# Seven-product columns widened from 512 to 680, over chains of two PSUM banks, in a quantised-weight FFN kernel

## What is computed

```python
lora_delta = lora_B @ lora_A * (LORA_ALPHA / LORA_RANK)
normalized = (weight + lora_delta).reshape(O, I // GROUP, GROUP) / scale
idx = jnp.searchsorted(thresholds, normalized, side='left')
w_eff = (cb[idx] * scale).reshape(O, I) + lora_delta
c = x @ w_eff.T                      # the conditioning product
result = jnp.einsum('bsd,od->bso', c, W_base) + b_base
ax, probs = einsum(c, A_w), softmax(einsum(c, router_w))
x = x + result + einsum(mixed(ax, probs, cores), B_w) * SCALING
```

## Time and profile before

| | |
|---|---|
| median of 3 runs | 2316.75 us (2315.3 to 2317.07) |
| the profiled execution's own time | 2317.91 us |
| its span, first to last instruction | 2316.1 us |
| mean granted clock of TensorE | 0.993 |
| PE busy, share of the span | 97% |
| DVE busy, share of the span | 85% |
| pairs 2 to 14 of stage 1, 13 pairs | 938.42 to 1213.16 us |

### The profile page before, as it was taken

How to read it: one execution, slowest core, us unless ns; L and a number is a source line. 1 busy time by engine, 2 the same in 40 slices (tenths; PEclk the granted TensorE clock), 3 DMA queues, 4 the chain that set the end, 5 groups by cost and what they waited for, 6 DMA issues and landing times.

```text
span 2316.1 us, 31908 instructions
## 1 busy us (share of the span) xinstructions
PE 2240.4 (97%) x11610; PEld 2022.0 (87%) x11610; DVE 1969.0 (85%) x2509; ACT 1496.5 (65%) x1962; POOL 1381.3 (60%) x894
## 2 busy tenths in 40 slices
PE   3889899999999999999999999999999999999999
PEld 2445479999999989899999989899999999999998
DVE  8999998889997977999997988999996766777776
ACT  7999978989886765666664865666663664122121
POOL 6888846669874534888775635887872132333231
PEclk9999999999999999999999999999999999999999
DMA  5787855444434434666664334666656666646554
GB/s 208 261 287 274 313 211 178 163 147 156 149 129 141 116 109 177 234 239 248 246 229 156 116 105 173 226 247 253 248 211 201 186 189 186 240 190 229 194 218 155
DMA packets 133234, 459.63 MB, mean 198 GB/s; under 512 B 14114, under 2 KB 66914, under 8 KB 96354
## 3 DMA queue, kind: packets, MB, share of 16 engines
q1 hardware_dynamic: 133076, 457.59, 56.7%
HBM read 306.41 MB, written 151.13 MB: 198 GB/s over the span
## 4 chain that ended last, share of the span: by engine, by line
PE 85%; DVE 9%; ACT 3%; DMA 1%; issue 1%; POOL 0%; DVEq 0%; SPq 0%; POOLq 0%; ACTq 0%
PE m L1239 6%; PE m L1238 6%; PE m L1240 6%; DVE acc L1713 6%; PE m L1190 5%; PE m L1192 5%; PE m L1191 5%; PE m L1296 4%; PE m L1298 4%; PE m L1297 4%; PE m L1346 4%; PE m L1348 4%; PE m L1347 4%; PE m L1131 4%; PE m L1307 3%; PE m L1306 3%
## 5 line engine op out<-in xcount | busy, mean ns | idle before, releaser
L1713 DVE SCALAR_TENSOR_TENSOR acc<-mk,dj,acc 128x1024 f32<-128x1024 uint8 x736 | 943.2, 1282 | 66.3 <-ACT mk L1461 47.9
L1461 ACT ACTIVATE mk<-wr,bj 128x1024 uint8<-128x1024 f32 x736 | 811.7, 1140 | 3.0 <-DVE acc L1713 2.1
L2034 POOL TENSOR_TENSOR pp<-pp,tm 128x1024 f32<-128x1024 f32 x184 | 454.0, 2468 | 22.3 <-POOL tm L2020 0.6
L2020 POOL TENSOR_SCALAR tm<-mp,dj 128x1024 f32<-128x1024 uint8 x192 | 226.0, 1178 | 211.0 <-ACT mp L1467 203.5
L1817 DVE TENSOR_TENSOR kl<-kw,kh 128x416 fp32r<-128x416 f32 (+3 forms) x310 | 237.6, 775 | 85.8 <-ACT kh L1496 84.7
L1496 ACT ACTIVATE kh<-kw 128x416 fp32r<-128x416 f32 (+3 forms) x310 | 169.1, 548 | 182.1 <-DMA kw<-in_wb 91.8
L1239 PE MATMUL m<-gl,xh 128*128 128x384 f32 (+2 forms) x800 | 280.9, 351 | 0.0
L1238 PE MATMUL m<-gh,xh 128*128 128x384 f32 (+2 forms) x800 | 280.6, 351 | 0.0
L1240 PE MATMUL m<-gh,xl 128*128 128x384 f32 (+2 forms) x800 | 279.8, 350 | 0.0
L1467 ACT ACTIVATE mp<-wr,bj 128x1024 uint8<-128x1024 f32 x224 | 255.1, 1139 | 0.0
L1773 DVE TENSOR_TENSOR part<-m,part 128x512 f32<-128x512 f32 (+4 forms) x362 | 217.6, 610 | 30.9 <-PE m L1240 16.6
(11 more groups left out here) (249 smaller groups left out, 5169.8 us busy)
## 6 DMA issues: line engine op xcount, KB each, us to landing
part<-part SPq DMA_DIRECT2D x191, 1036.0 KB, 4.8
rows<-in_wb SPq DMA_DIRECT2D x61, 1036.0 KB, 4.8
out<-part SPq DMA_DIRECT2D x31, 1024.0 KB, 4.8
kw<-in_ws SPq DMA_DIRECT2D x128, 208.0 KB, 2.7
xw<-in_x SPq DMA_DIRECT2D x96, 256.0 KB, 3.3
kw<-in_wb SPq DMA_DIRECT2D x92, 192.0 KB, 2.4
wr<-in_w SPq DMA_DIRECT2D x32, 512.0 KB, 5.9
dl<-delta SPq DMA_DIRECT2D x30, 512.0 KB, 5.3
```

Of the source, the lines that this page charges most:

```text
L1461: e.activation(R.mk[m % NM], w, ACT.Identity, bias=R.bj[:, j:j + 1], scale=GROW).then_inc(S["mk"], 1)
L1713: e.scalar_tensor_tensor(R.acc, R.mk[m % NM], R.dj[:, j:j + 1], R.acc, ALU.mult, ALU.add).then_inc(S["ac"], 1)
L2034: e.tensor_tensor(R.pp, first, R.tm[scaled_level(q, i)], ALU.add).then_inc(S["pp"], 1)
```

## The change

`SW` goes from 512 to 680. A product is wider than a bank, so its chain covers two: `CHAIN_AT` puts the 680 columns at columns 172 and 1196 of banks `m0` to `m3` taken as one tile, with the border in the middle, and each matmul becomes two of 340. The rest of a half is 356 columns, two "rest" units per token in place of three, in the banks `m4` and `pd`. Which of the two chains a product takes changes with the pair's parity (`unit_chain`). The last pair is mixed too (`MIX_LAST`), the first and the last pair have an order of units of their own, and the low part of the second token moves from POOL to DVE (`second_low`, L1836), that of the token sums from DVE to POOL.

```diff
-SW = 512
-REST = (HX - SW) // 3 * 2
-MIX = (("prod", 1), ("prod", 2), ("rest", 0, 0), ("rest", 0, 1), ("prod", 6), ("prod", 5), ("rest", 0, 2), ("prod", 7),
-       ("prod", 3), ("rest", 1, 0), ("prod", 4), ("rest", 1, 1), ("rest", 1, 2))
+SW = 680
+SPLIT_SW, REST = 340, HX - SW
+CHAIN_AT = (512 - SPLIT_SW, 3 * 512 - SPLIT_SW)
+MIX = (("prod", 1), ("prod", 2), ("rest", 0, 0), ("prod", 6), ("prod", 5), ("rest", 0, 1), ("prod", 7), ("prod", 3),
+       ("rest", 1, 0), ("prod", 4), ("rest", 1, 1))
+MIX_END = (("prod", 1), ("rest", 0, 0), ("prod", 5), ("prod", 6), ("rest", 0, 1), ("prod", 3), ("prod", 7), ("rest", 1, 0),
+           ("prod", 2), ("prod", 4), ("rest", 1, 1))
-MIX_FIRST, MIX_LAST = 1, PAIRS - 2
+MIX_FIRST, MIX_LAST = 1, PAIRS - 1
-WAIT_LEVELS, END_LEVELS, WAIT_SLOTS = 8, 11, 4
+WAIT_LEVELS, END_LEVELS, WAIT_SLOTS = 14, 9, 4
...
-            if at == (11 if mixed(p) else 9) and mixed(p + 1):
+            if at == (MIX_OF[p].index(("prod", 3)) + 2 if mixed(p) else 9):
                 yield ("token_sums_high", g, p + 1)
-                if p:
-                    yield ("token_sums_low", g, p + 1)
+                yield ("token_sums_low", g, p + 1)
...
+def unit_chain(u):
+    return (u[0] + (u[2] in (2, 3, 5))) % 2
+def unit_banks(u):
     if u[1] == "prod":
-        return 1 if u[2] in (2, 3, 5) else 0
-    return 2 + (6 * u[0] + 3 * u[2] + u[3]) % 4
+        return {2 * unit_chain(u), 2 * unit_chain(u) + 1}
+    return {NCH - 1 + u[3]}
...
+            pieces = ((0, SPLIT_SW), (SPLIT_SW, SW))
             for kp in range(2):
-                e.matmul(bank[:, 0:SW], high, oh, start=kp == 0 and n in (1, 2, 5), stop=False, skip_group_check=n in (3, 4, 6, 7))
+                for c0, c1 in pieces:
+                    e.matmul(R.mm[:, first + c0:first + c1], high, oh[:, c0:c1], start=kp == 0 and n in (1, 2, 5), stop=False,
+                             skip_group_check=n in (3, 4, 6, 7))
...
+    def second_low(g, t):
+        xw, xl, xh = R.token(g, t)
+        e.wait_ge(S["xh"], NT * g + t + 1)
+        e.wait_ge(S["qs"], 4 * sums_count(g, t // 2))
+        e.tensor_tensor(xl, xw, xh.bitcast(F32), ALU.subtract).then_inc(S["xd"], 1)
...
+            e.wait_ge(S["mc"], multiplied(g, PAIR_FIRST[g][MIX_FIRST] - 1))
             rebuilt(3, 1, 0)
```

More of the change, by code:

```diff
@@ L524, in first_at_home @@
 def first_at_home(g, s):
-    guests = {**GUEST, **(GUEST_LAST if g == LAST else {})}
-    return s not in guests and all(k in guests for k in range(s % RING, s, RING))
+    return s not in GUEST[g] and all(k in GUEST[g] for k in range(s % RING, s, RING))
 def wait_consumed(e, S, q):
@@ L556, in units_of_stage @@
         if mixed(p):
-            units += [(p, *u) for u in MIX]
+            units += [(p, *u) for u in MIX_OF[p]]
         else:
@@ L603, in prod_unit, with half_done_at, bank_last @@
 def prod_unit(g, p, n):
-    return PAIR_FIRST[g][p] + MIX.index(("prod", n))
+    return PAIR_FIRST[g][p] + MIX_OF[p].index(("prod", n))
+def half_done_at(p):
+    if not mixed(p):
+        return NCH
+    return 1 + max(k for k, u in enumerate(MIX_OF[p]) if unit_tokens((p, *u))[0] == (0,))
+def bank_last(g, v):
+    return max(k for k, u in enumerate(UNITS_OF[g]) if v in unit_banks(u))
 def multiplied(g, k):
@@ L615, in bank_before @@
 def bank_before(g, k):
[L617 removed]
+    return max((j for j in range(k) if unit_banks(UNITS_OF[g][j]) & unit_banks(UNITS_OF[g][k])), default=None)
 def target_before(g, k):
@@ L631, in sums_free, with low_by_vector, pool_lows, vector_lows @@
 def sums_free(g):
-    return multiplied(g, prod_unit(g, MIX_LAST, 3))
+    return multiplied(g, max(prod_unit(g, MIX_LAST, n) for n in (3, 5, 6, 7)))
+def low_by_vector(g, t):
+    return g in MIXED and mixed(t // 2) and t % 2 == 1
+def pool_lows(g, t):
+    places = [(i, u) for i in range(g + 1) for u in range(NT) if (i, u) <= (g, t)]
+    return sum(1 for i, u in places if not low_by_vector(i, u))
+def vector_lows(g, t):
+    return NMIX * (g - 1) + t // 2 - MIX_FIRST + 1
+def wait_low(e, S, g, t):
+    if low_by_vector(g, t):
+        e.wait_ge(S["xd"], vector_lows(g, t))
+    else:
+        e.wait_ge(S["xl"], pool_lows(g, t))
 def x_buffer(g, t):
@@ L1295, in mul @@
                 oh, ol = sum_operand(n, kp, False), sum_operand(n, kp, True)
-                e.matmul(bank[:, 0:SW], high, oh, start=kp == 0 and n in (1, 2, 5), stop=False, skip_group_check=n in (3, 4, 6, 7))
-                e.matmul(bank[:, 0:SW], high, ol, start=False, stop=False, skip_group_check=n in (3, 4, 6, 7))
-                done = e.matmul(bank[:, 0:SW], low, oh, start=False, stop=kp == 1, skip_group_check=n in (3, 4, 6, 7))
+                for c0, c1 in pieces:
+                    e.matmul(R.mm[:, first + c0:first + c1], high, oh[:, c0:c1], start=kp == 0 and n in (1, 2, 5), stop=False,
+                             skip_group_check=n in (3, 4, 6, 7))
+                for c0, c1 in pieces:
+                    e.matmul(R.mm[:, first + c0:first + c1], high, ol[:, c0:c1], start=False, stop=False,
+                             skip_group_check=n in (3, 4, 6, 7))
+                for c0, c1 in pieces:
+                    done = e.matmul(R.mm[:, first + c0:first + c1], low, oh[:, c0:c1], start=False, stop=kp == 1,
+                                    skip_group_check=n in (3, 4, 6, 7))
         else:
@@ L1937, in vector_program @@
                 mul_added(at[0], at[1] - 1)
+        elif what == "x_low":
+            if low_by_vector(*at):
+                second_low(*at)
         elif what == "spread":
@@ L2170, in gpsimd_program @@
                 clear()
-        elif what == "x_split" and at[0] and at[1] < 2 or what == "x_low":
+        elif what == "x_split" and at[0] and at[1] < 2:
             split_x(*at)
+        elif what == "x_low":
+            if not low_by_vector(*at):
+                split_x(*at)
         elif what == "late_normalised":
@@ L2176, in gpsimd_program @@
             token_sums(*at)
+        elif what == "token_sums_low":
+            token_sums_low(*at)
         elif what == "close":
```

172 lines of the change are left out of this document (90 added, 82 removed), and 2 rows, old and new, of the table COMPUTE.

## The result

The kernel after takes 2331.15 us, median of 4 runs (2329.12 to 2332.83), the kernel before 2316.91 (2315.3 to 2317.57) beside it: ratio 1.0065, 95% interval 1.0050 to 1.0079. It is slower by 14 us; the forecast was 9 us faster. The profiled execution has a span of 2328.7 us at a granted clock of 0.994.

What follows compares the result with a forecast made beforehand. PE, busy 97% of the span, was taken as the bound, with DVE close behind. 12.0 - 1.0 - 1.2 - 0.5 = 9.3 us off the profiled 2317.9 gave 2308.6, median 2307.5, range 2303.5 to 2312.

Steps and rivals of the forecast that it cites:

- It is hidden under PE, but with 0.5 us a pair to catch up in: Mixed pairs: DVE's 20.3 us of work fits under PE's 20.83 us, 97.5% full.
- The matmuls: Fourteen mixed pairs in two stages: each 0.30 us shorter, 20.83 us, a gain of 8.4 us.
- Pair 15 and the ends: Last pair, now mixed, takes 20.83 for 22.61 us, gaining 3.6 in two stages; low parts at stage ends lose 0.5.
- The start: Start of the mixed pairs: PE waits for DVE 2.8 us a stage, 5.6 against 4.4, a loss of 1.2 us.
- The bound of 7 us: Start of the mixed pairs: upper bound on the loss a stage, if all DVE's 1360 wide instructions are stretched.
- DVE: Usual mixed pair: DVE's work sums to 20.3 us of 20.83, with `xl` taken at 1.15.
- The range of 0.6 to 1.55: Usual mixed pair: time in us of DVE's `xl`, from half the extremes of `sl`; 1.15 was taken.
- DVE becomes the bound: Rival, mixed pairs: `xl` at 1.7 us or more; at 2.0 PE loses 9.2 us, start 4 more: 2320.7; chance 0.08.
- POOL: Mixed pairs: POOL's work rises from 17.4 by 1.8 to 19.2 of 20.83 us a pair.
- Late token sums: Mixed pairs: DVE's `xl` waits for POOL's sums, 1 us allowed; as rival, in most pairs, 14 us: 2321, chance 0.10.
- narrow pieces no cheaper: Rival, matmuls: narrow pieces cost as much as 344 wide ones, gain 3 us, median 2314; chance 0.12.
- a floor of weight loads: Rival, matmuls: weight loads hold each at 0.174 us, new pair 23.0 us, kernel 2370; chance 0.02.

Runs made afterwards that it cites:

- part_behind_x: Kernel after, with the load of the second token's old part moved on SP's queue behind the next x load: 2314.0 us.
- round_later: Kernel after, with ACT's rounding of the second token's x moved from unit 4 to 7 and DVE's low part from 7 to 8: 2309.56 us.
- both_and_pool: Kernel after with the changes of part_behind_x and round_later, and the second token's low part of x on POOL in four pairs a stage: 2305.16 us.
- levels_three_quarters: Kernel after, work left out: DVE's accumulation of levels from half 17 on covers 768 of 1024 columns: 2313.9 us.
- before_x_late: Kernel before, with the second token's x load in mixed pairs moved on SP behind the load of part[2p+2]: 2490.28 us.

## Why the prediction was wrong

**The step that failed** is the sentence "It is hidden under PE, but with 0.5 us a pair to catch up in". It looked at DVE's own sum and not at what DVE's time feeds. The prediction has no term for the load of x at all: SP's queue is not in it, though `half_done` and `fetch_ahead` move by a unit and `xl` was placed ahead of the addition on which the store waits. The runs put in its place a lap of five members: DVE's last addition of a token, its store, the load into its buffer, x behind that load, ACT's rounding with the masks behind. Cutting in at SP gave 17.2 us back, at another queue 17.4, at ACT 20.7, at DVE's order 16.7, each alone.

**The matmuls** (8.4 us): right in kind. An undisturbed pair is 20.87 for 20.83, so 28 x 0.26 = 7.3 us.

**Pair 15 and the ends** (3.6 - 0.5): 21.5 and 21.1 where 22.61 was in both stages, 2.6 us in all.

**The start** (2.8 a stage over a usual pair): pair 1 took 22.4 in both stages, 1.55 over. The bound of 7 us was far off.

**DVE** (20.3 us of 20.83): the term that was too small is `xl`, taken at 1.15. Its group by form over the span, in the kernel after, in part_behind_x, in round_later and in both_and_pool (mean ns behind the comma):

```profile
L1836 DVE TENSOR_TENSOR xl<-xw,xh 128x512 fp32r<-128x512 f32 x30 | 43.3, 1443 | 1.5 <-POOL sf L2132 1.5
L1835 DVE TENSOR_TENSOR xl<-xw,xh 128x512 fp32r<-128x512 f32 x30 | 47.6, 1588 | 5.7 <-POOL sf L2131 5.7
L1837 DVE TENSOR_TENSOR xl<-xw,xh 128x512 fp32r<-128x512 f32 x30 | 38.4, 1279 | 0.0
L1838 DVE TENSOR_TENSOR xl<-xw,xh 128x512 fp32r<-128x512 f32 x22 | 24.9, 1132 | 0.0
```

At unit 7 it takes 1.44 to 1.59 on average, and DVE had 20.86 us a pair in part_behind_x; at unit 8 it takes 1.28, and without four of the pairs of a stage 1.13. The range of 0.6 to 1.55 had the 1.44 of the kernel after but not the 1.59 of part_behind_x; the value taken had neither. So this is a second step that failed, by its size: in pairs 2 to 14 of part_behind_x `xl` takes 1.66, 0.5 more than reckoned, as much as the whole room to catch up in. The rival *DVE becomes the bound* held in part. It gave a loss of 9.2 us in the pairs and 4 at the start; part_behind_x, with the lap gone, has 13.5 us of excess against 6.6 forecast.

**POOL** (19.2 us a pair): 247.56 / 13 = 19.0. **Late token sums**, 1 us: the sums ended no later than 16.1 us into a pair in both stages, and in the whole stretch DVE waited for them 1.5 us. That rival's mechanism did not act. But it shared the right worry: `xl` at unit 7 standing ahead of product 3's addition. What it held up there was the store, not the next chain.

**The sum again:** 2307.5 + 1.1 (pairs) + 0.5 (ends) - 2.5 (start) + 25.2 (pairs 2 to 14 beyond the 1.0 allowed) = 2331.8, and 2331.15 was measured. The loss in it is the measured one, so the sum explains nothing by itself, and that it comes within 0.7 us is in part luck: in spans these parts make 14.8 us where 12.6 were measured, and 1.6 of the difference lie ahead of pair 1 (912.84 for 914.41), 0.9 in the weight stage between the two; no run shows why. The other rivals, narrow pieces no cheaper and a floor of weight loads, are ruled out by the spacing of 0.156. The chance of 0.15 for slower was too low, since the cases on that side, but for the floor of weight loads, needed DVE to be held up by what it does itself; none had a late x.

Why the kernel before keeps x in time with 0.7 us of spare DVE time a pair, while the kernel after with over 2 us (levels_three_quarters) doesn't, can be read at SP. The kernel before at the border of pairs 5 and 6 of stage 1, which lies at 1022.96:

```profile
1017.21 0.32 SPq L909 DMA_DIRECT2D part<-part  x1
1022.93 0.32 SPq L898 DMA_DIRECT2D part<-part  x1
1023.29 0.43 SPq L891 DMA_DIRECT2D xw<-in_x  x1
```

There the even token's store goes out 5.75 us ahead of the next pair (5.1 to 6.2 at 24 borders), about what it takes to land, so x goes out with the pair's start (0.2 to 0.3 us in). In the kernel after it is 1.9 us ahead (0.1 to 3.3) and x 3.0 us in (1.5 to 5.7); in levels_three_quarters 2.3 and 2.0. So the room that counts is that of the store ahead of the pair's end, and the change took most of it. What stays open is how much of this the shift of the issues by a unit, the place of `xl` and the shorter pair took each: no run separates them.

## What to carry to other kernels

Before an engine is loaded to within a few per cent, follow its last instruction of each round through the queues: which store waits for it, which loads stand behind that store in an in-order queue, and who stands still for them. If the way leads back to the engine, spare time must be counted around the whole lap. Put what isn't urgent (a rounding whose input is late, a low part) behind the masks and additions that others wait for: here moving one rounding by three units was worth 20.7 us, and cost nothing that the time shows.

## What the runs showed of the hardware

DVE's subtraction of two 128x512 tensors in SBUF takes between 0.68 and 2.7 us in the kernel after. One line of the kernel after over the span (ns min/median/max), and then DVE and POOL in one place of stage 1:

```profile
L1836 DVE TENSOR_TENSOR xl<-xw,xh x30: 676/1326/2708, 910.7 to 1746.5; 128x512 fp32r<-128x512 f32 x30
...
953.78 2.63 DVE L1836 TENSOR_TENSOR xl<-xw,xh 128x512 fp32r<-128x512 f32 x1
...
953.46 2.40 POOL L2103 TENSOR_TENSOR wr<-wr,dl 128x1024 f32<-128x1024 f32 x1
```

POOL's two-operand instruction ends at 955.86; DVE's, started 0.3 us behind it, at 956.41. Less 0.68 that is 955.73, as if it had stood still till POOL was done. It is so throughout: of the 30 in the kernel after, five took 0.68 us and the other 25 all end 0.54 to 0.55 us behind the end of a POOL instruction that ran beside them (in 4 of the 25 a POOL instruction with a single tensor operand). The Trainium skill (Trainium Architecture — The Big Picture, What this means for kernel authors) has it that of the engines only DVE and GpSimd contend for SBUF, by a port pair that one of them holds alone; the rows agree, though no run here isolates it. DVE's additions of 680 columns, which read PSUM for one operand, took 0.85 to 0.87 us in all 210 instances. It fits that the same `xl` has a mean of 1.59 in one order and 1.13 in another: what matters is which POOL instruction it falls beside and how much of that is still to run, and a price taken from stage 0 (1.22) is that of another neighbourhood.

A load of x (128x512 f32) issued at 1071.02 let ACT go on at 1077.40, 6.4 us later; the stores of whole rows of `part` took 4.5 and 6.0 us from their issue to that of the load behind. The granted clock of PE was 0.91 in the stretch of before_x_late whose pairs had gaps of 2 to 7 us, and 1.00 in pairs 2 to 14 of the kernel after, whose gaps were at most 1.9 us.
